# A style-conditioned convolution chain and two adapters: the order of the demodulation at the start, the first fold ahead of layer 1, and three products of a cleared tile

## The reference

```python
s = style @ mw.T + mb
weight = SCALE * w * s[:, None, :, None]
demod = lax.rsqrt(jnp.sum(weight * weight, axis=(2, 3)) + EPS)
weight = weight * demod[:, :, None, None]
...
x = x + _L0_ffn_ref(_L0_cond_ref(x, cond_512, ...), L0_ffn_A, L0_ffn_B, L0_ffn_Wr)
x = x + _L1_ffn_ref(_L1_cond_ref(x, cond_512, ...), L1_ffn_qweight, L1_ffn_scales, L1_ffn_zeros, L1_ffn_bias)
```

## Time and profile before

| | us |
|---|---|
| Time, median of 3 runs | 926.48 |
| lowest, highest | 926.36, 927.63 |
| Profiled execution, its own time | 927.74 |
| Its span in the trace | 926.1 |
| PE busy in the span | 915.6 |
| DVE busy | 494.0 |
| ACT busy | 409.2 |

### The profile page before, as it was taken

The page is one execution under the profiler, slowest core; times in us unless marked ns, Lnnn a source line. Parts: engine busy times, 40 slices in busy tenths (PEclk is TensorE's granted clock), DMA queues, the critical chain, the costliest instruction groups (busy, mean ns, idle before and its releaser), DMA issues.

```text
span 926.1 us, 14642 instructions
## 1 busy us (share of the span) xinstructions
PE 915.6 (99%) x5024; PEld 824.7 (89%) x5024; DVE 494.0 (53%) x1078; ACT 409.2 (44%) x764; POOL 92.4 (10%) x115
## 2 busy tenths in 40 slices
PE   7999999999999999999999999999999999999998
PEld 6889889899899899898898898988998999998998
DVE  7885434334345245244254365587665566666555
ACT  5943323423333343244243235386545565655540
POOL 0000000000000000000000030312111121111121
PEclk9999999999999999999999999999999999999999
DMA  8801101101101102011011011333122221122111
GB/s 286 274 11 59 68 23 45 68 17 51 47 21 68 45 23 68 23 45 68 23 45 68 23 57 69 41 128 101 69 80 81 91 91 68 68 76 83 69 69 69
DMA packets 33132, 64.29 MB, mean 69 GB/s; under 512 B 11728, under 2 KB 14032, under 8 KB 33104
## 3 DMA queue, kind: packets, MB, share of 16 engines
q1 hardware_dynamic: 24032, 30.90, 11.0%
q0 software_dynamic: 9072, 33.03, 9.5%
HBM read 47.14 MB, written 16.78 MB: 69 GB/s over the span
## 4 chain that ended last, share of the span: by engine, by line
PE 92%; DVE 4%; ACT 2%; issue 1%; DMA 0%; DVEq 0%; ACTq 0%
PE conv_ps L180 9%; PE conv_ps L182 9%; PE conv_ps L181 9%; PE fold_ps L786 6%; PE prod_ps L976 5%; PE prod_ps L977 5%; PE prod_ps L978 5%; PE prod_ps L943 5%; PE prod_ps L945 5%; PE prod_ps L944 5%; PE prod_ps L1052 4%; PE prod_ps L1051 4%; PE fold_ps L751 3%; PE turn_ps L897 3%; PE turn_ps L945 2%; PE turn_ps L943 2%
## 5 line engine op out<-in xcount | busy, mean ns | idle before, releaser
L166 DVE TENSOR_TENSOR h_lo<-conv_ps,h_hi 64x512 fp32r<-64x512 f32 x128 | 88.3, 690 | 47.2 <-ACT h_hi L850 46.1
L180 PE MATMUL conv_ps<-h_hi,e_hi 128*128 128x512 f32 x256 | 103.7, 405 | 0.6 <-DVE h_lo L166 0.5
L181 PE MATMUL conv_ps<-h_lo,e_hi 128*128 128x512 f32 x256 | 101.8, 398 | 0.0
L182 PE MATMUL conv_ps<-h_hi,e_lo 128*128 128x512 f32 x256 | 101.7, 397 | 0.0
L870 ACT ACTIVATE cond<-conv_ps,bias,demod_tab 128x510 f32<-128x510 f32 x64 | 49.8, 778 | 102.6 <-PE conv_ps L182 102.5
L976 PE MATMUL prod_ps<-b_hi,xt 128*128 128x512 f32 x240 | 93.5, 389 | 0.0
L977 PE MATMUL prod_ps<-b_lo,xt 128*128 128x512 f32 x240 | 93.4, 389 | 0.0
L978 PE MATMUL prod_ps<-b_hi,xt 128*128 128x512 f32 x240 | 93.4, 389 | 0.0
L943 PE MATMUL prod_ps<-a_hi,xt 128*128 128x384 f32 x240 | 81.1, 338 | 0.0
L945 PE MATMUL prod_ps<-a_hi,xt 128*128 128x384 f32 x240 | 81.1, 338 | 0.0
L944 PE MATMUL prod_ps<-a_lo,xt 128*128 128x384 f32 x240 | 81.0, 338 | 0.0
(11 more groups left out here) (301 smaller groups left out, 2160.3 us busy)
## 6 DMA issues: line engine op xcount, KB each, us to landing
x_in<-in_x SPq DMA_DIRECT2D x64, 128.0 KB, 2.7
res<-in_x POOLq DMA_DIRECT2D x16, 512.0 KB, 3.5
x_after_first<-res POOLq DMA_DIRECT2D x16, 512.0 KB, 2.9
x_in<-x_after_first SPq DMA_DIRECT2D x64, 128.0 KB, 2.7
res<-x_after_first POOLq DMA_DIRECT2D x16, 512.0 KB, 3.5
out_x<-res POOLq DMA_DIRECT2D x15, 512.0 KB, 3.0
a_raw<-in_adapter_in SPq DMA_DIRECT2D x8, 544.0 KB, 8.7
b_raw<-in_adapter_out SPq DMA_DIRECT2D x8, 512.0 KB, 12.2
```

The lines of the kernel that those rows point to most:

```text
L166: return nc.vector.tensor_tensor(out, whole, hi.bitcast(F32), ALU.subtract)
L180: nc.tensor.matmul(out, hi(w), moving_hi(i), start=(i == 0), stop=False)
L181: nc.tensor.matmul(out, hi(w), moving_lo(i), start=False, stop=False)
L182: last = nc.tensor.matmul(out, lo(w), moving_hi(i), start=False, stop=(i == n - 1))
```

## The change

For level 0 the demodulation is cut in three: layer 2 first (32 columns), with `scale3` right behind it; then, after `v_lo` is made, layers 0 and 1 (64 columns) with `scale1` and `bias1`; then, after `r_lo`, layer 3 (32 columns), and only behind that `bias_vector`. `scale2`, which needs only styles, is made before all of it and has a semaphore of its own. The low part of the layer-2 weights (`raw_lo` "f3") moves behind `scale3`. ACT evicts fold3 (`act_fold3`) ahead of the first `act_layer1`, and DVE makes `r_lo` ahead of `bias_vector`, the low part of the upsample weights (`head_lo`) and the border step. PE begins with three products of a cleared 128x128 tile (fp32, 256 columns, into conv_ps[1], which the first real product there overwrites); DVE clears the tile as its first instruction. The load of the second adapter matrix waits for `demod_ready` in place of `tables_ready`. In level 1 the demodulation stays whole; only `scale2` stands ahead of it instead of behind.

```diff
@@ new and changed helpers
-            V.tensor_scalar(s.var[:, :], tables_ps[L][:, 256:256 + LAYERS * B], SCALE * SCALE, EPS, ALU.mult, ALU.add)
-            link(v, V.reciprocal(demod, s.root[:, :]))
...
+            cols = slice(layers.start * B, layers.stop * B)
+            demod = demod_tab[:, :, :].rearrange("o l b -> o (l b)")[:, cols]
+            var, newton = s.var[:, cols], s.newton[:, cols]
+            V.tensor_scalar(var, tables_ps[L][:, 256 + cols.start:256 + cols.stop], SCALE * SCALE, EPS, ALU.mult, ALU.add)
+            link(v, V.reciprocal(demod, s.root[:, cols]))
+            link(v, V.tensor_tensor(newton, demod, demod, ALU.mult))
+            link(v, V.tensor_tensor(newton, newton, var, ALU.mult))
+            link(v, V.tensor_scalar(newton, newton, -0.5, 1.5, ALU.mult, ALU.add))
+            return V.tensor_tensor(demod, demod, newton, ALU.mult)
+
+        def fold_tables(v, L, s):
+            v.wait_ge(S.root_ready, L + 1)
             if L:
-                bias_vector(v, L, s)
+                link(v, demod_vector(v, L, s, slice(0, LAYERS)))
+            else:
+                link(v, demod_vector(v, L, s, slice(2, 3)))
+            nc.vector.tensor_tensor(scale3[:, :], demod_tab[:, 2, :], style_tab[:, 3, :], ALU.mult).then_inc(S.scale3_ready, 1)
+
+        def layer1_tables(v, L, s):
+            V = nc.vector
+            if not L:
+                link(v, demod_vector(v, L, s, slice(0, 2)))
+            V.tensor_tensor(scale1[:, :], demod_tab[:, 0, :], demod_tab[:, 1, :], ALU.mult)
+            V.tensor_scalar(bias1[:, :], demod_tab[:, 1, :], bias_of(s, 0), None, ALU.mult).then_inc(S.tables_ready, 1)
@@ tensor
+            pe.wait_ge(S.blank_ready, 1)
+            for _ in range(3):
+                nc.tensor.matmul(conv_ps[1][:, 0:2 * P], blank, blank.unsqueeze(1).broadcast_to([P, 2, P]), start=True, stop=True)
             style_tensor(pe, 0, set0)
@@ scalar
             act_fold_start(act, 0, buf0, True)
+            act.wait_ge(S.scale2_ready, 1)
+            act_fold3(act, 0, buf0, True)
             act.wait_ge(S.tables_ready, 1)
             act_layer1(act, 0, 0, buf0)
-            act_fold3(act, 0, buf0, True)
             act.wait_ge(S.sides_cleared, 1)
@@ vector
+            nc.vector.memset(blank, 0.0).then_inc(S.blank_ready, 1)
...
             tap_sums_vector(v, set0)
+            scale2_vector(v)
             dve_split(v, 0, 0, buf0, True)
+            fold_tables(v, 0, set0)
             raw_lo(v, 0, set0, "f3")
-            tables_vector(v, 0, set0)
             dve_fold_start(v, 0, buf0)
+            layer1_tables(v, 0, set0)
             dve_split(v, 0, 1, buf0, True)
+            dve_fold3(v, 0, buf0)
+            link(v, demod_vector(v, 0, set0, slice(3, 4)))
+            v.sem_inc(S.demod_ready, 1)
             bias_vector(v, 0, set0)
             head_lo(v, set0)
             head_edge_vector(v, set0, 1)
-            dve_fold3(v, 0, buf0)
             dve_layer1(v, 0, 0, buf0)
```

More of the change, by code:

```diff
@@ L88, in program @@
         S.down_ready = sem("down_ready")
-        S.scale3_ready = sem("scale3_ready")
+        S.scale2_ready, S.scale3_ready, S.demod_ready = sem("scale2_ready"), sem("scale3_ready"), sem("demod_ready")
         S.a_hi_ready, S.a_lo_ready = sem("a_hi_ready"), sem("a_lo_ready")
@@ L94, in program @@
         S.pads_ready = sem("pads_ready")
+        S.blank_ready = sem("blank_ready")
         S.tiles_cleared = sem("tiles_cleared")
@@ L568, in clear_squares, with demod_vector @@
                 nc.vector.memset(s.style_sq[h * C:(h + 1) * C, :, 1 - h, :], 0.0)
-        def tables_vector(v, L, s):
-            n = L + 1
+        def demod_vector(v, L, s, layers):
             V = nc.vector
-            v.wait_ge(S.root_ready, n)
-            demod = demod_tab[:, :, :].rearrange("o l b -> o (l b)")
-            V.tensor_scalar(s.var[:, :], tables_ps[L][:, 256:256 + LAYERS * B], SCALE * SCALE, EPS, ALU.mult, ALU.add)
-            link(v, V.reciprocal(demod, s.root[:, :]))
[L578 to L587, removed]
-            if L:
-                bias_vector(v, L, s)
@@ new lines, in layer1_tables, with scale2_vector @@
+        def layer1_tables(v, L, s):
[4 more added lines that the diff above has]
+            V.tensor_scalar(bias1[:, :], demod_tab[:, 1, :], bias_of(s, 0), None, ALU.mult).then_inc(S.tables_ready, 1)
+        def scale2_vector(v):
+            nc.vector.tensor_tensor(scale2[:, :], style_tab[:, 1, :], style_tab[:, 2, :], ALU.mult).then_inc(S.scale2_ready, 1)
@@ L1115, in program @@
         setup_kept(level0, 1, set1)
+        blank = buf0.res[:, 0:P]
         buf0.gated = buf0.cond[:, :, :].rearrange("p a h -> p (a h)")
@@ L1203, in _ @@
             sp.wait_ge(S.style_done, 1)
-            sp.wait_ge(S.tables_ready, 1)
+            sp.wait_ge(S.demod_ready, 1)
             sp.wait_ge(S.turn_blurred, 1)
@@ L1586, in _ @@
             act_fold_start(act, c, slot(c), True)
+            act.wait_ge(S.scale2_ready, 2)
             act.wait_ge(S.tables_ready, 2)
@@ L1762, in _ @@
             split(NPAIR, slot(NPAIR), True)
-            tables_vector(v, 1, set1)
+            scale2_vector(v)
+            fold_tables(v, 1, set1)
+            layer1_tables(v, 1, set1)
+            bias_vector(v, 1, set1)
             dve_fold_start(v, NPAIR, slot(NPAIR))
```

## The result

The changed kernel takes 931.11 us, the median of five executions (929.56 to 931.65), where the kernel before took 926.47 (926.36 to 927.63, five executions) on the same chip: a ratio of 1.0048, with a 95% interval of 1.0037 to 1.0059. (The ratios given in this text are not quotients of the medians and differ from them by up to 0.0007.) It is slower, by 4.6 us, and above the range of the prediction. The profiled execution of the changed kernel is the one of 931.11 us; its span is 929.4.

What follows compares the result with a forecast made beforehand. PE's order up to fold2 was taken as the bound. Fold2 1.9 us later through PE's wait for the bias, added to the median 926.48, gave 928.4 us; the other parts cost nothing at the end. Range 926.3 to 930.4.

Steps and rivals of the forecast that it cites:

- What bounds the kernel: PE up to fold2 (19.12 us): what fold2 loses or gains passes one for one to the first loop and the end.
- Cleared tile and three products: PE's start: three products take 2.6 to 2.9 us, end at 4.1 to 4.3, making the styles 0.1 late.
- Layer 2 first: Level 0 on DVE and ACT: a 32-column chain of 1.38 us lets v_hi start at 12.19, 1.27 earlier.
- x_lo, r_lo: DVE after the chain for layers 0 and 1: r_lo starts at 16.1 and is ready at 17.0, 2.1 us earlier.
- Layer 3's demodulation ahead of the bias: DVE delays inner_ready to 18.55, PE waits 2.9 us at the bias product, fold2 starts at 21.0, 1.9 later.
- The clock in the wait: PE's wait for the bias: the forecast (chance 0.45) counted no fall of the clock in the 2.9 us.
- rival 2: Clock falls in PE's wait; blur and fold2 at half speed, at most 3.9 us more, half taken: 930.4; chance 0.13.
- Rival 1: Clock rises early, at about 5 to 6 us, after the three products; fold2 at 20.3, 927.7 us; chance 0.25.
- Rivals 3 and 4: 3: bias does not hold up PE, fold2 0.9 earlier, 925.6, chance 0.07; 4: loss absorbed before loop, 926.5, chance 0.10.

Runs made afterwards that it cites:

- e11: The changed kernel itself, run again on another chip beside the kernel before: 929.83 us, ratio 1.0038.
- e2: The changed kernel without the clearing of the tile and the three products: 931.33 us, ratio 1.0048 to the kernel before.
- e3: The changed kernel with six more products of the cleared tile on PE, between border product and bias product: 929.36 us, ratio 1.0021 to the kernel before.
- e1: The changed kernel with bias_vector moved ahead of the second x_lo, so ahead of layer 3's demodulation: 927.19 us, ratio 1.0008 to the kernel before.
- e5: The changed kernel with PE doing the blur of the turned weights ahead of the bias product: 927.2 us, ratio 1.0004 to the kernel before.
- e8: The changed kernel with layer 3's demodulation made twice on DVE ahead of the bias, same values: 932.76 us, ratio 1.0055 to the kernel before.
- e4: The kernel before with only the clearing of the tile and the three products added: 927.02 us, ratio 1.0 to the kernel before.
- e9: The changed kernel with bias_vector and head_lo both ahead of layer 3's demodulation: 927.78 us, ratio 1.0013 to the kernel before.

## Why the prediction was wrong, point by point

**What bounds the kernel: right.** PE's time without work in the first 20 us is passed on one for one: the gates moved by 4.99 us with a late fold2 of 4.25 and slower first products of it (0.75 more up to the bias product behind them), by 1.89 in e11 with fold2 1.83 late.

**Cleared tile and three products: right.** Forecast to end at 4.1 to 4.3, they end at 4.22.

**Layer 2 first: the number right, the path not.** v_hi was forecast at 12.19 and starts at 12.23, in e11 at 12.24. The prediction had it wait for scale3, but scale3 was done at 11.27 (11.08 + 0.19), in e11 at 11.98. What v_hi waited for is ACT's own work ahead of it, the second half of x, which stands behind a `fold_hi` that waits for PE's blur of `L_up`; DVE idled 1.10 us over it:

```profile
11.34 0.39 ACT L382 ACTIVATE fold_hi<-fold_ps 128x256 fp32r<-128x256 f32 x1 [1.87 <-PE fold_ps L376]
11.62 0.71 ACT L831 ACTIVATE x_hi<-x_in,style_tab 128x513 fp32r<-128x513 f32 x1
```

That the time agrees to 0.04 is luck. It cost nothing, since fold3 had to wait for PE's layer-1 products in any case. The prices were right: the chain priced at 1.38 took 1.37 (9.71 to 11.08), that of 64 columns, priced at 1.70, took 1.72 (13.39 to 15.11). (In the bounds of the forecast, 2 x 1.04 + 0.72 is 2.8 and not 2.7, and half of the 0.45 is 0.22 and not 0.24; neither changes the forecast.)

**x_lo, r_lo: right.** r_lo was forecast at 16.1 to 17.0; in e11 it stands at 16.03 to 16.90.

**Layer 3's demodulation ahead of the bias: right, and the cause of the loss.** inner_ready was forecast at 18.55 and came at 18.79, in e11 at 18.55; PE's wait at 2.9 and measured 2.89; fold2 at 21.0, which e11 has at 20.95 and e2 and e3 at 20.74. e1 shows the cause by moving it, e5 by letting PE pass it, e3 gives its price as 1.7 to 2.2, and e8 shows that the wait grows with the chain.

**The clock in the wait: the step that failed.** The forecast took the clock as held, gave rival 2 a chance of 0.13, and priced it at "half, 2.0". In the first set it fell in the profiled execution, and by their times (930.92 to 931.65) in three more of five. e3, where PE is fed in the wait, has no such execution in eleven: the fall needs the wait. And its price is not a half but nearly all: the bias product and the blur ran wholly at the low level (18.84 to 23.37 is 4.53, against 2.45 in the earlier trace rows), 2.1 us more, fold2's first products lost 0.75, and the wait itself ended 0.26 later than forecast, since the first products of fold3 were still at the low level (fold3 took 1.48 us, 13.66 to 15.14, and 1.15 in e11): 3.1 us, where 3.9 was named as the most. Rival 2 with this measured price is 926.5 + 1.9 + 3.1 = 931.5, where four of the five executions lie. The reason for the 0.13 was that the earlier trace rows shows no fall in a wait of 0.83; a row about a wait a third as long says nothing about 2.9. The text held both bounds of the unknown, 0 and 3.9, and cut the range at half.

**Rival 1, the early rise: it came in some executions and gained nothing.** It came from the rule of the Trainium skill, "TensorE: Matmul & The Clock Gate", Part 1, that the default is throttled and activity releases it. The traces agree in part: of the ten with the three products five (the changed kernel, e1, e4, e5, e9) have the high level by 5.5 to 6 us (1.00 against 1.81 us for the eight records of the down blur), the other five have not, and neither has any of the three without them. The line on warming up in the table of the Trainium skill, "TensorE: Matmul & The Clock Gate", "Why this matters for your kernels", which the prediction names, has measuring a matmul accurately as its goal, not making a kernel faster. What was gained is lost again: the record is low from about 8 to 14. PE waits for loads around there, 0.42 and 1.53 us, but in e1 it is busy when the level falls, so what brings this fall isn't shown. fold3 starts at 13.66 with the early rise and at 13.67 in e11 without it; only in e5, where the low stretch ends at 12, does it start at 13.14. Rival 1's 927.7 was met by nothing.

**The late dip: a term that was missing.** The sum stood on a profiled execution with a dip of 1.5 us near 643, where the granted clock is 0.83 for 640 to 650. It does not change the difference between like executions, but it changes which ones a median falls on: 8 of the 21 of before beside e11 have its mean clock, and all five of e11.

**Rivals 3 and 4: rightly small.** With the bias out of the way (e1, e5, e9) nothing was gained: the border step and L_inner on DVE come late next. And the loss was not taken up ahead of the loop.

**Open.** Why the clock holds through waits of 2.97 (e11) and 3.10 us (e2) and falls two microseconds into one of 2.89 isn't shown. In the traces here, it fell in that wait once, in an execution in which it had also been low from 8 to 14, and held twice in executions in which the record stands at 1.00 from 8 to 14. That is no rule: e8's fell, just behind the wait, with 1.00 there, and the slow executions of e2 have a mean clock of 0.996 where the two low stretches of the changed kernel's profiled one make 0.993, so they have room for one only. Nor is it shown why the late dip comes in some executions.

## What to carry to other kernels

When work moves on a helper engine, look for the first small operation behind it that the main engine waits for, and move that ahead, or let the main engine pass the wait (e5): here moving three operations of 0.24 us was worth about 4 us. Price a new wait of TensorE twice, once as its length and once with all the work behind it at the low clock, until a trace shows that the clock holds in a wait of that length; a row about a shorter wait doesn't. And before a sum is made against a profiled execution, compare its granted clock over the whole span with the other executions': a dip elsewhere is a term of its own.

## What the hardware showed that I had not expected

- The clock can fall or hold in the same wait of the same program: four executions of five near 931 in the first set, five of five near 929.8 in the last. Once it had fallen it stayed at 0.50 from about 18 to past 24 us, although PE was busy without a gap from 18.84.
- A fall need not come while PE is idle: in e1 the record falls at 7.7 with PE busy from 5.96 to 8.05, in e8 at 20.1, just behind a wait of 4.49 us in which it stood at 1.00, and in before at 642.7, behind 18 products of 32 columns.
- The record of the granted clock and the spacing of products disagree at the start: 1.00 in the earlier trace rows with products of 512 columns 0.43 apart, while an execution in which the level had risen and fallen has 0.50 there with the same 0.43. At the very start only the spacing tells the level.
- A kernel with PE busy 99% has a dip of 1.5 us at 643 us in its profiled execution, and the mean clock that goes with it in about half of all; it makes two groups of times about 1.5 us apart, wider than most of what was measured here.
